# Loading 40 tiles of x one by one inside the first layer's tile loop

## The reference

```python
h = jnp.maximum(_layernorm(x, axis=-1), 0.0)
for l in range(3):                                   # first network
    xr = jnp.einsum('nd,rde->rne', h, W_rel[l])      # a table of 8 products for each node
    agg = segment_sum(xr[edge_type, src], dst)       # gathered and summed by destination
    h = relu(agg + h @ W_root[l] + bias[l])
x = x + h
h = jnp.maximum(_layernorm(x, axis=-1), 0.0)
h = h @ Wv + bv;  q = h @ wq + bq;  k = h @ wk + bk  # second network
c = leaky_relu(q[src] + k[dst], 0.2)
attn = softmax of c over the edges of each dst
x = x + segment_sum(h[src] * attn, dst)
```

## Time and profile before

| | us |
|---|---|
| median of 3 runs (4722.2 to 4723.2) | 4723.12 |
| the profiled execution: device time | 4725.13 |
| its span (first to last instruction) | 4723.3 |
| of the span: first stage up to the first gather | 377.0 |
| the four gather passes and the end | 4346.3 |

### The profile page before, as it was taken

How to read it: one execution, slowest core, us unless ns; L and a number is a source line. 1 busy time by engine, 2 the same in 40 slices (tenths; PEclk the granted TensorE clock), 3 DMA queues, 4 the chain that set the end, 5 groups by cost and what they waited for, 6 DMA issues and landing times.

```text
span 4723.3 us, 61500 instructions
## 1 busy us (share of the span) xinstructions
PE 3631.8 (77%) x12856; PEld 2476.4 (52%) x12857; DVE 1146.8 (24%) x3241; ACT 2002.3 (42%) x5249; POOL 3296.4 (70%) x3465
## 2 busy tenths in 40 slices
PE   8997888888887888888886666666664667666676
PEld 3444555555554555555554444444443555555555
DVE  2330000000000000000001111111114666666665
ACT  2334444444543544545453343444442444344343
POOL 1136777777775777777776777777776777777775
PEclk9998999999988998989897888877777888888888
DMA  6345555454544444444443444444443333333332
GB/s 221 160 170 166 162 158 164 155 165 155 164 155 136 158 157 151 158 149 158 149 158 112 116 118 117 117 117 117 117 116 90 105 105 106 104 106 104 107 106 80
DMA packets 231629, 640.95 MB, mean 136 GB/s; under 512 B 60406, under 2 KB 105911, under 8 KB 212740
## 3 DMA queue, kind: packets, MB, share of 16 engines
q0 software_dynamic: 160336, 439.40, 32.6%
q10 hardware_dynamic: 42264, 128.52, 7.4%
q1 hardware_dynamic: 28956, 72.34, 4.0%
HBM read 466.54 MB, written 173.49 MB: 136 GB/s over the span
## 4 chain that ended last, share of the span: by engine, by line
POOL 66%; issue 21%; PE 10%; DMA 1%; SPq 1%; DVE 0%; ACT 0%; DVEq 0%; POOLq 0%; ACTq 0%
POOL ring L477 66%; PE bank L1124 8%; PE sum_ps L1205 1%; DMA ring<-table,code 0%; DMA table<-stage 0%; SPq L546 0%; PE turn_ps L1114 0%; PE sum_ps L1300 0%; DMA features<-xT 0%; PE sum_ps L1198 0%; DMA ring<-h_table,code 0%; ACT xT L906 0%; SPq L548 0%; DVE z L716 0%; SPq L536 0%
## 5 line engine op out<-in xcount | busy, mean ns | idle before, releaser
L477 POOL DMA_INDIRECT ring<-table,code x2496 | 2368.8, 949 | 860.1 <-issue 830.4
L1205 PE MATMUL sum_ps<-ring,masks 128*128 x5586 | 1410.8, 412 | 253.5 <-SPq L572 232.4
L1205 PEld LDWEIGHTS sum_ps<-ring,masks 128*128 128x128 f32 x5586 | 1140.5, 207 | 518.0 <-issue 346.0
L1124 PE MATMUL bank<-wide,xT 128*128 128x512 f32 (+1 forms) x2744 | 1255.9, 616 | 176.2 <-issue 164.8
L477 POOL DMA_INDIRECT ring<-h_table,code x832 | 859.1, 1033 | 272.2 <-issue 272.2
L1124 PEld LDWEIGHTS bank<-wide,xT 128*128 128x128 f32 x2744 | 556.0, 208 | 822.2 <-issue 815.7
L990 ACT ACTIVATE masks<-node_row,local 128x128 f32<-128x128 f32 x2793 | 831.5, 387 | 345.0 <-issue 271.1
L913 ACT COPY stage<-bank 128x512 f32<-128x512 f32 x441 | 257.6, 585 | 766.2 <-PE bank L1124 766.2
L1300 PE MATMUL sum_ps<-ring,stage 128*128 x1862 | 512.1, 424 | 0.5 <-ACT stage L1075 0.5
L1300 PEld LDWEIGHTS sum_ps<-ring,stage 128*128 128x128 f32 x1862 | 384.8, 218 | 53.6 <-issue 0.9
L630 DVE COPY stage<-bank 128x512 f32<-128x512 f32 x147 | 101.7, 692 | 1266.6 <-PE bank L1124 1266.6
(11 more groups left out here) (142 smaller groups left out, 1484.7 us busy)
## 6 DMA issues: line engine op xcount, KB each, us to landing
table<-stage ACTq DMA_DIRECT2D x98, 1024.0 KB, 4.6
table<-stage SPq DMA_DIRECT2D x49, 1024.0 KB, 3.8
ring<-table,code POOLq DMA_INDIRECT x2496
ring<-h_table,code POOLq DMA_INDIRECT x832
h_table<-stage ACTq DMA_DIRECT2D x49, 130.0 KB, 2.3
features<-xT SPq DMA_DIRECT2D x49, 128.0 KB, 3.6
first_T<-features ACTq DMA_DIRECT2D x49, 128.0 KB, 4.3
wide<-in_L_gnn_W_rel_dram SPq DMA_DIRECT2D x6, 1024.0 KB
```

The lines of the kernel that those rows point to most:

```text
L477: pool.indirect_dma_start(slot(c % RING, width), None, table, bass.IndirectOffsetOnAxis(ap=code[:, c:c + 1], axis=0)).then_inc(landed[n % ...
L1124: last = nc.tensor.matmul(bank[q][:, 0:width], xT[:, b, k, :], weights[:, k, 512 * q:512 * q + width], start=(k == 0), stop=(k == K - 1))
L1205: last = nc.tensor.matmul(sum_ps[b][:, 0:D], masks[:, b, s, :], at_offset(slots[s]), start=(s == 0 and l > 0), stop=(s == SLOTS - 1))
```

## The change

The single load of tiles 9 to 47 and the load of tile 48 ahead of the loop are gone. SyncE's loop now issues, behind the stores of tile i, the load of tile i+9, for i from 0 to 37; tiles 47 and 48 are loaded between the first loop (19 pairs) and a second one with the other pairs. Even and odd ones count on two semaphores, `x_later0` and `x_later1`, and each load waits until the one before it on its semaphore has landed. VectorE waits from pair 4 on for each tile ahead of its statistics, where it waited once. GpSimd's edge loads wait for the weights and tiles 0 to 8 only. `CREDIT` is 1; SOME is 9 and LATER is 20.

```diff
-            pool.wait_ge(x_rest, 32)
+            pool.wait_ge(weights_loaded, 16 * (2 * K + 1))
+            pool.wait_ge(x_some, 16)
...
+            def load_later(i, j, b, last=False):
+                rows = LAST if last else P
+                base = (NT - 1) * P if last else i * P
+                sp.wait_ge(x_later[b], 16 * CREDIT + 16 * j)
+                sp.dma_start(root[0:rows, i, :], x[bass.ds(base, rows), :]).then_inc(x_later[b], 16)
+
             load_start(0, 1, x_first)
             load_weights(0)
-            load_start(1, some, x_some)
-            if some < NT - 1:
-                load_start(some, NT - 1, x_rest)
+            load_start(1, SOME, x_some)
             sp.wait_ge(consts_ready, CONSTS)
-            sp.dma_start(root[0:LAST, NT - 1, :], x[(NT - 1) * P:N, :]).then_inc(x_rest, 16 if some < NT - 1 else 32)
...
-            over_tiles(sp, before_layers)
+            with sp.Fori(0, LATER - 1) as j:
+                before_layers(2 * j, j, 0)
+                load_later(SOME + 2 * j, j, 0)
+                before_layers(2 * j + 1, j, 1)
+                load_later(SOME + 2 * j + 1, j, 1)
+            load_later(NT - 2, LATER - 1, 0)
+            load_later(NT - 1, LATER - 1, 1, last=True)
+            with sp.Fori(LATER - 1, PAIRS) as j:
+                before_layers(2 * j, j, 0)
+                before_layers(2 * j + 1, j, 1)
+            before_layers(NT - 1, PAIRS, 0)
...
+            def wait_later(j, b):
+                if not all_loaded[0]:
+                    dve.wait_ge(x_later[b], 16 * CREDIT + 16 * (j - SOME // 2 + 1))
...
             def pair_before_layers(j):
+                wait_later(j, 0)
                 first_norm(2 * j + 1, j, 1)
                 evacuate(2 * j, j, 0, first=True)
+                wait_later(j, 1)
                 first_norm(2 * j + 2, j + 1, 0)
                 evacuate(2 * j + 1, j, 1, first=True)
```

More of the change, by code:

```diff
@@ L198, in gnn_program @@
         weights_loaded = sem("weights_loaded")
-        x_first, x_some, x_rest = sem("x_first"), sem("x_some"), sem("x_rest")
+        x_first, x_some = sem("x_first"), sem("x_some")
+        x_later = sems("x_later", 2)
         x_loaded = sems("x_loaded", 2)
@@ L298, in gnn_program @@
         plan_rows = plan[:, :].rearrange("p (t s) -> p t s", s=PLAN)
+        SOME = min(9, NT // 2 | 1)
+        LATER = (NT - SOME) // 2
         FIRST_STEP = 7 if PAIRS >= 20 else 1
@@ L308, in before_layers_at @@
             first = 0
-            for pair, step in steps:
+            for pair, step in sorted(steps, key=lambda placed: placed[0]):
                 if pair > first:
@@ L537, in load_start @@
                              ).then_inc(arrives, 16)
-            some = min(9, NT - 1)
+            def load_later(i, j, b, last=False):
[3 more added lines that the diff above has]
+                sp.dma_start(root[0:rows, i, :], x[bass.ds(base, rows), :]).then_inc(x_later[b], 16)
             load_start(0, 1, x_first)
             load_weights(0)
-            load_start(1, some, x_some)
-            if some < NT - 1:
-                load_start(some, NT - 1, x_rest)
+            load_start(1, SOME, x_some)
             sp.wait_ge(consts_ready, CONSTS)
-            sp.dma_start(root[0:LAST, NT - 1, :], x[(NT - 1) * P:N, :]).then_inc(x_rest, 16 if some < NT - 1 else 32)
             for row, of in ((bv_row, bv), (wq_row, wq), (wk_row, wk)):
@@ L604, in _ @@
                 nc.vector.memset(credit[:, k:k + 1], 0.0).then_inc(counted_by_one, CREDIT)
-            by_dma = (*stored, *h_stored, *out_stored, *features_stored)
+            by_dma = (*stored, *h_stored, *out_stored, *features_stored, *x_later)
             for k, counted_by_dma in enumerate(by_dma, len(by_one)):
@@ L640, in first_norm, with from_here_later @@
                 normalise(root[:, i, :], j, b)
+            all_loaded = [True]
+            def wait_later(j, b):
+                if not all_loaded[0]:
+                    dve.wait_ge(x_later[b], 16 * CREDIT + 16 * (j - SOME // 2 + 1))
+            def from_here_later():
+                all_loaded[0] = False
             def pair_before_layers(j):
+                wait_later(j, 0)
                 first_norm(2 * j + 1, j, 1)
                 evacuate(2 * j, j, 0, first=True)
+                wait_later(j, 1)
                 first_norm(2 * j + 2, j + 1, 0)
@@ L679, in _ @@
             before_layers_at(dve, pair_before_layers, (
-                (4 if PAIRS >= 20 else 0, lambda: dve.wait_ge(x_rest, 32)), (place(0), chunk_ranges), (place(1), keep_code),
+                (SOME // 2, from_here_later), (place(0), chunk_ranges), (place(1), keep_code),
                 (place(1), count_below), (place(6), any_broken), (place(10), plan_sums)))
```

## The result

The changed kernel takes 4713.56 us (median of 22 runs), the kernel before 4723.47 (22 runs beside it): ratio 0.9976, 95% interval 0.9970 to 0.9982. That is 9.9 us between the medians, where 6.85 were forecast. The profiled execution has a span of 4710.7 us against 4723.3: 12.6, so 2.7 of that difference are more than the medians show.

A forecast was written before the change was run, and what follows sets the result against it. The first stage was taken as bound by TensorE except for one wait for ScalarE's ReLU of tile 2. Removing it gave -6.85 us, all other parts nothing: 4723.12 - 6.85 = 4716.3 us, range 4712 to 4722.

The forecast's parts named there:

- the side that was given 0.09: Whole time: chance of being faster by over 0.2%, which needs 9.4 us.
- The wait goes wholly: First stage: TensorE's wait for ScalarE's ReLU of tile 2, behind tile 0's features store, vanishes; -6.85 us.
- the term of 6.85: Turns around tile 2: 13.94 us against a steady 7.09, made of 4.90 idle and 1.95 at the lower clock.
- The start, between nothing and 1.7: First matmul's wait for weights until 11.4: moving the large load could free bandwidth, 0 to 1.7 us; taken as nothing.
- The edge loads: GpSimd's edge loads come 17 us earlier, beside tile 0's features store; at worst 0.1 us plus a little clock, taken as nothing.
- Forty loads in the loop, two between the loops: SyncE's queue: 0.33 us issue and 0.3 transfer per load; features store of tile 38 4.2 us late, cover 7.5; no cost.
- The rule on the fixed part of a DMA: Some 2.0 us fixed per DMA: 38 more DMAs carry 76 us, an estimated 4792 us if all on the path.
- The slower rival: Loads crowd the stores in SyncE's queue; 3.6 us per load gives +17.5 us, 4740.6, deciding from 2.96 us; chance 0.05.
- The passes: Gather passes: 4346 us of unchanged instructions, with 2 us either way allowed for another build.

The follow-up runs named there:

- a2: Changed kernel with extra register instructions in the gather passes, GpSimd's edge loads held until tile 10 of x; 4721.89 us, 0.9990 of the plain kernel before.
- c4_before: Kernel before with one register instruction added to each awaited semaphore value in the gather passes; 4726.57 us, 1.0008 of the plain kernel before.
- a1: Changed kernel with one register instruction added to each awaited semaphore value in the gather passes; 4722.09 us, 0.9993 of the plain kernel before.
- a3: Kernel before with the extra register instructions, only GpSimd's edge loads moved early, single large load kept; 4737.24 us, 1.0022 of the plain kernel before.
- b2: Changed kernel with the extra register instructions and 1024 KB more behind each of the loop's 38 loads; 6035.49 us, one run on a slower chip.
- b3: Changed kernel with the extra register instructions and 1536 KB more behind each of the loop's 38 loads; 6055.82 us, one run on a slower chip.
- c0_after: Changed kernel with the extra register instructions, run on a slower chip; 5995.3 us, 0.9954 of the plain kernel before there.
- b1_large_behind: Kernel before with the extra register instructions, single large load issued behind tile 0's features store; 6044.06 us, beside 6008.19 of the plain kernel before.

## Why the prediction was right, and where it was small

The forecast was 4716.3 us in a range of 4712 to 4722, and a change within 0.2% was given 0.86. The time is 4713.56: in the range, and the mechanism is the one forecast. The gain, 0.24% with an interval of 0.18 to 0.30%, is clear of no change and lies on the side that was given 0.09. Of the 9.9 us the first gather accounts for 8.

*The wait goes wholly.* Right. No wait is left but the two at the start, the turns are 7.09 apart, and a2 shows that the moved loads do it alone. Between the turns of tiles 2 and 3, three executions of the kernel before show 13.94, 15.72 and 13.28 us, and those of the changed one 7.08 to 7.09. So the term of 6.85 is one draw of a wait that costs 6.2 to 8.6 us: 4.90, 5.6 and 4.23 idle, and 1.95, 3.0 and 2.0 for the lower clock (the second wait left twelve rows of 8.14 us). The mean of the three is 7.2; c4_before's 6.2 is also less than the 6.9 to 8.7 that was expected of it.

*The rest of the 7.98 us at the first gather.* The turns of tile 1 stand at 19.14 before and 18.38 after, 0.76 us that no part of the change explains, and that is luck: in the programs with the register instruction the same turn falls between 18.7 and 20.0 whichever kernel it is, since the first twelve rows take 7.0 to 8.4 us. The step from the last table store to the first gather is shorter by 0.36 (5.76 for 6.12). That one is no chance, since it returns in every pair, and the prediction has no term for it. What goes with it is the later issue of the next layer's weights; that these take transfer time from the store is not tested. 6.85 + 0.76 + 0.36 = 7.97.

*The start, between nothing and 1.7.* Nothing: the first matmul stands at 11.41 before and at 11.55 after. The large load took nothing from the weights in front of it. The bound of 1.7 counted tile 0 twice: without it 2432 KB are left, 6.5 us at 381 GB/s, and the bound is 1.9.

*The edge loads.* I took them at nothing, which is right for the changed kernel (a2 and a1 agree). That this rests on the large load being gone is what a3 shows, where the same step costs 3.9 us at the first gather; the prediction named the sharing, and bounded it for this kernel only.

*Forty loads in the loop, two between the loops.* Nothing, as forecast. The features store of tile 38 was issued 5.5 us behind the table store, in place of 1.3: 4.2 us late, as worked out, and within its cover. Against the 0.53 of the earlier trace rows it is 5.0: a load in front costs the features store more than the 0.33 us of issue that I took, and its own issue lasts 0.69 or 1.09 us in the loop, where it was 0.33. The cover bore that too. The rule on the fixed part of a DMA, from the Trainium skill, DMA: Bandwidth & Descriptors, "Anatomy of one DMA", does not bear on the path here: the forty loads, of which one in the loop takes 3.7 us to land, and 38 of them with a further 1024 KB behind each, left the first gather at 369.02 and 369.81.

*The slower rival.* Its mechanism was right, and its edge wrong: it was put at 2.96 us of queue time for a load, from the landing times, and b2 passed with a further load of 1024 KB, 2.7 us at 382 GB/s, on top of the tile's own; b3 with 1536 KB lost 18 us where the same reckoning gave 65, and the bytes at 382 GB/s give 17.5.

*The passes.* I allowed 2 us, and named passes that no longer take 4346 us as a sign of being wrong. In the profile after they take 4341.7. Of the 12.6 us between the first two spans 4.8 arise in the last pass (1111.3 and 1106.6 us). That the change does this is not shown, and that it is chance is likely, but not shown either: the seven profiles with the register instruction and passes of this length have the last pass at 1111.2 to 1117.9, and the same program twice differs by up to 3.9 us, but 1106.6 lies below all of them. The spread itself is the gathers': those of over 1.1 us number 134 to 156 in the last pass, and of the 11.4 us between the shortest and the longest pass 10.7 are in their excess over 0.95 us, 62 to 73 us in all. What makes a gather slow I haven't tried.

The three pairs of medians put the gain at 9.9, 7.1 and 8.0 us. The first gather, which the passes don't blur, puts it at 7.98, 7.96 and 6.94. What stays open is whether the 9.9 of the plain kernels holds 2 us that the other programs on that chip don't show, or chance: the interval there begins at 8.5 us. The 17.4 us of c0_after leave the same question open.

## What to carry to other kernels

A large load that nobody needs yet costs by what stands behind it in its queue: look for the small store or load behind it that frees a buffer. Moving the large one back by one store only moved the wait to the next tile and shortened it here, from 4.9 to 2.94 us; cutting it up took the wait away, since a queue with room carries many small loads at no cost. Room is a matter of bytes: count those of a tile, not the times to landing. A wait removed from a busy TensorE also returns time at the lower clock, and that part differs from one execution to the next, so give such a term a width. Where a change is below the scatter of the whole time, read the gain at the event that ends the changed stage, in several profiles.

## What the runs showed of the hardware

- The clock's part of a wait is uneven: after idle times of 4.23, 4.90, 5.6 and 10.24 us the next twelve rows took 7.11, 7.11, 8.14 and 7.61 us, at a mean granted clock of 0.76, 0.76, 0.66 and 0.70, and 5.41 us at 1.00 after 2.94 us, where twelve rows at the higher clock take some 5.3.
- The issue of the DMA right behind the 4992 KB load holds SyncE: 14.63 us, 14.65 in b1_large_behind, 19.20 with GpSimd's loads beside it, and at most 2.32 at the head of the profile after. So a long issue here says what stands in front, and whatever stands behind it in the queue waits too.
- SyncE's queue moved 382 GB/s over 220 us, loads and stores mixed, and only there did TensorE wait for stores. At 330 GB/s with the DMA engines 99% busy it didn't: the busy share alone doesn't tell that a queue is at its end.
